# Graph layer on one core: degree count within the first half of G, its second half evicted scaled, norm's small matmuls spread over the blocks

## What is computed

```python
Q = relu(x @ Wq + bq);  V = x @ Wv + bv
# gcn: G = x @ Wg, summed over edges with both degrees' roots
deg  = segment_sum(ones, dst) + 1            # one self loop a node
dinv = rsqrt(max(deg, 1e-12))
gcn  = segment_sum(G[src] * dinv[src] * dinv[dst], dst) + self loop + bg
# former: Q = relu(layer_norm(Q)); H = a scaled square of Q's row sums
cosQ, sinQ = Q * cos(H), Q * sin(H)
out  = (cosQ @ (cosQ.T @ V) + sinQ @ (sinQ.T @ V)) / norm
norm = cosQ @ sum(cosQ) + sinQ @ sum(sinQ) + 1e-10
y = relu(layer_norm(out + gcn + V, gamma, beta))
return layer_norm(x + y)
```

## Time and profile before

| | us |
|---|---|
| median of three runs | 1887.72 |
| lowest and highest run | 1881.73, 1896.17 |
| the profiled execution | 1891.69 |
| its span in the trace | 1889.8 |

### The profile page before, as it was taken

How to read it: one execution, slowest core, us unless ns; L and a number is a source line. 1 busy time by engine, 2 the same in 40 slices (tenths; PEclk the granted TensorE clock), 3 DMA queues, 4 the chain that set the end, 5 groups by cost and what they waited for, 6 DMA issues and landing times.

```text
span 1889.8 us, 27579 instructions
## 1 busy us (share of the span) xinstructions
PE 1642.4 (87%) x7707; PEld 1252.9 (66%) x7707; DVE 1585.2 (84%) x4322; ACT 953.7 (50%) x1789; POOL 1038.4 (55%) x1106
## 2 busy tenths in 40 slices
PE   5888974999999997788888879999899898988995
PEld 4566652777777775565556667767677776777774
DVE  7999975899889897787777878888689888887886
ACT  2222213555555555555555556656456555554554
POOL 0000006777777777677787758878445444444440
PEclk8999985999999999899999989999899898998998
DMA  6445578899888998677777858878566676675762
GB/s 218 160 159 176 173 271 267 281 307 302 290 289 304 302 302 264 196 233 231 247 237 238 246 185 258 257 246 269 167 202 206 197 220 197 195 210 167 220 189 88
DMA packets 179601, 433.16 MB, mean 229 GB/s; under 512 B 24558, under 2 KB 26218, under 8 KB 179432
## 3 DMA queue, kind: packets, MB, share of 16 engines
q0 software_dynamic: 71120, 233.10, 41.0%
q1 hardware_dynamic: 87180, 159.65, 24.8%
q10 hardware_dynamic: 21132, 38.50, 5.5%
HBM read 354.13 MB, written 77.03 MB: 228 GB/s over the span
## 4 chain that ended last, share of the span: by engine, by line
DVE 37%; PE 31%; DMA 11%; issue 7%; ACT 6%; POOL 5%; SPq 1%; DVEq 1%; ACTq 0%; POOLq 0%
DVE stage L787 7%; PE bank L1104 6%; PE bank L1105 6%; PE bank L1106 6%; PE bank L1188 5%; DMA rows<-scaled_g,index_slots 5%; DMA split<-scaled_g,index_slots 5%; PE bank L1190 5%; DVE split L832 4%; POOL split L441 3%; DVE rows L832 3%; DVE stage L783 3%; ACT split L518 3%; DVE one_hot L828 2%; DVE stage L1046 2%
## 5 line engine op out<-in xcount | busy, mean ns | idle before, releaser
L441 POOL DMA_INDIRECT split<-scaled_g,index_slots x490 | 531.5, 1085 | 334.1 <-PE bank L1190 212.4
L441 POOL DMA_INDIRECT rows<-scaled_g,index_slots x392 | 423.8, 1081 | 174.3 <-PE bank L1190 80.0
L1188 PE MATMUL bank<-split,one_hot 128*128 128x512 f32 x882 | 380.5, 431 | 120.4 <-DVE split L832 62.8
L518 ACT CAST split<-split 128x512 fp32r<-128x512 f32 x490 | 301.3, 617 | 356.1 <-PE bank L1190 185.5
L832 DVE TENSOR_TENSOR split<-split 128x512 fp32r<-128x512 f32 x490 | 336.8, 687 | 86.1 <-ACT split L518 84.4
L518 ACT CAST split<-rows 128x512 fp32r<-128x512 f32 x392 | 240.7, 617 | 275.7 <-PE bank L1190 177.2
L1104 PE MATMUL bank<-weights,operands 128*128 128x512 f32 x784 | 323.4, 412 | 4.2 <-DMA operands<-turned_x 4.2
L1188 PEld LDWEIGHTS bank<-split,one_hot 128*128 128x128 f32 x882 | 170.3, 193 | 233.7 <-DVE rows L832 109.0
L1106 PE MATMUL bank<-weights,operands 128*128 128x512 f32 x784 | 317.3, 405 | 0.0
L1105 PE MATMUL bank<-weights,operands 128*128 128x512 f32 x784 | 316.9, 404 | 0.0
L832 DVE TENSOR_TENSOR rows<-rows,split 128x512 fp32r<-128x512 f32 x392 | 270.0, 689 | 50.9 <-ACT split L518 49.3
(11 more groups left out here) (201 smaller groups left out, 2553.9 us busy)
## 6 DMA issues: line engine op xcount, KB each, us to landing
turned_x<-operands SPq DMA_DIRECT2D x49, 512.0 KB, 3.0
operands<-turned_x SPq DMA_DIRECT2D x49, 512.0 KB, 5.9
stage<-values SPq DMA_DIRECT2D x98, 256.0 KB, 4.1
stage<-in_x SPq DMA_DIRECT2D x96, 256.0 KB, 2.7
scaled_g<-nodes SPq DMA_DIRECT2D x49, 256.0 KB, 3.4
own_rows<-scaled_g SPq DMA_DIRECT2D x49, 256.0 KB, 4.1
values<-stage ACTq DMA_DIRECT2D x49, 256.0 KB, 4.1
combine<-values SPq DMA_DIRECT2D x49, 256.0 KB
```

The costliest lines, as they stand in the source:

```text
L441: pool.indirect_dma_start(out=plain(row_ring[k % RING]), out_offset=None, in_=table, in_offset=bass.IndirectOffsetOnAxis(ap=index_slots[:, ...
L518: act.copy(hi_ring[k % SPLIT], plain(row_ring[k % RING])).then_inc(s["chunk_rounded"], 1)
L1188: pe.matmul(gcn_banks[seq % 2][:, :], one_hot[:, slot, :], hi_ring[slot], start=k == 0, stop=False, skip_group_check=True)
```

## The change

- The degree count now takes two units of 18 chunks (10 and 8) a tile, so that 47 units are done within the first 24 tiles (HIST_TILES).
- A half unit's one-hots come from one comparison each on VectorE, against a written-out bf16 counter; the layout is now (j, c), the chunk c innermost. On TensorE the roles are swapped: the one-hot of 49 is the stationary side, that of 128 the moving one, both read at a step of 10 elements. The 49 x 128 result is copied and turned on TensorE.
- `dinv` is ready at tile 26. From tile 28 (SCALED) ScalarE evicts G already scaled; the 28 tiles before are scaled by VectorE, two behind each of tiles 27 to 40, and SyncE stores them two behind each of tiles 28 to 41, and the scaled ones with two tiles' delay. x has four slots from tile 28 on.
- The schedule's set-up moves to tiles 27 to 45, the low parts of Wq and Wv to tiles 3 to 17. The first loads of the QV stage (`first_x_load`) no longer wait for the last tile of G, and their slots in `operands` are other ones. TensorE's wait for `degrees_kept` ahead of QV is gone.
- In OUT, the two small norm matmuls of a block follow that block's products.

```diff
-    HIST = -(-CHUNKS // TILES)
+    HIST = 18
+    HALF = (10, 8)
+    UNITS = -(-CHUNKS // HIST)
+    HIST_TILES = -(-UNITS // 2)
+    SCALED = HIST_TILES + 4
...
             def g_keep(t, n, r):
                 act.wait_ge(s["g_summed"], done(t))
-                act.copy(tile_of(nodes, t)[0:r, :], banks[3 + n][0:r, :]).then_inc(s["g_kept"], 1)
-
+                if t < SCALED:
+                    act.copy(tile_of(nodes, t)[0:r, :], banks[3 + n][0:r, :]).then_inc(s["g_kept"], 1)
+                else:
+                    act.activation(tile_of(nodes, t)[0:r, :], banks[3 + n][0:r, :], ACT.Copy, scale=dinv[0:r, t:t + 1])                        .then_inc(s["g_kept"], 1)
...
+            def table_store(t):
+                if t < SCALED:
+                    sp.wait_ge(s["g_scaled"], t + 1)
+                else:
+                    sp.wait_ge(s["g_kept"], done(t))
+                sp.dma_start(dram_rows(table, t, P), tile_of(nodes, t)).then_inc(s["table_written"], 16)
...
+            for t in range(0, TILES):
+                if t <= WIDE:
+                    g_load(t + 2)
+                if t == WIDE:
+                    g_load(t + 3)
+                if t >= WIDE and t + 4 < TILES:
+                    g_load(t + 4)
+                xt_store(t)
+                if 0 <= t - SCALED < SCALED // 2:
+                    table_store(2 * (t - SCALED))
+                    table_store(2 * (t - SCALED) + 1)
+                if t - 2 >= SCALED:
+                    table_store(t - 2)
+            first_x_load(0)
+            first_x_load(1)
+            table_store(FULL - 1)
+            first_x_load(2)
+            table_store(FULL)
...
-                dve.tensor_tensor(div_hot[half][:, 0:count, 0:TILES],
-                                  iota_bf[:, 0:TILES].unsqueeze(1).to_broadcast([P, count, TILES]),
-                                  cols(dst_div).unsqueeze(2).to_broadcast([P, count, TILES]), ALU.is_equal)
-                for c in range(count):
-                    last = dve.tensor_scalar(mod_hot[half][:, c, :], iota_bf[:, :], column(dst_mod, c0 + c), None,
-                                             ALU.is_equal)
-                last.then_inc(s["bins_ready"], 1)
+                dve.tensor_tensor(div_hot[half][:, 0:TILES, 0:count], counter[:, 0:TILES, 0:count],
+                                  cols(dst_div).unsqueeze(1).to_broadcast([P, TILES, count]), ALU.is_equal)
+                dve.tensor_tensor(mod_hot[half][:, :, 0:count], counter[:, :, 0:count],
+                                  cols(dst_mod).unsqueeze(1).to_broadcast([P, P, count]), ALU.is_equal)\
+                    .then_inc(s["bins_ready"], 1)
...
-                    last = pe.matmul(banks[5][:, 0:TILES], mod_hot[half][:, c, :], div_hot[half][:, c, 0:TILES],
+                    last = pe.matmul(banks[5][0:TILES, 0:P], div_hot[half][:, 0:TILES, c], mod_hot[half][:, :, c],
                                      start=False, stop=False, skip_group_check=True)
...
                 g_product(t, n, r, [0, 1])
-                bins(t, 0)
+                if t < HIST_TILES:
+                    bins(2 * t, 0)
+                    bins(2 * t, 1)
                 g_product(t, n, r, [2, 3]).then_inc(s["g_summed"], 1)
-                bins(t, 1)
+                if t < HIST_TILES and 2 * t + 1 < UNITS:
+                    bins(2 * t + 1, 0)
+                    bins(2 * t + 1, 1)
...
             pe.wait_ge(s["raw_split"], 1 + 2 * B)
-            pe.wait_ge(s["g_kept"], done(FULL))
-            pe.wait_ge(s["degrees_kept"], 1)
...
-                            o_norms(n, slot)
-                            o_product(0, slot, [0, 1])
+                            for b in (0, 1):
+                                o_product(0, slot, [b])
+                                o_norms(n, slot, b)
                         if at == 1:
-                            o_product(0, slot, [2, 3])
+                            for b in (2, 3):
+                                o_product(0, slot, [b])
+                                last = o_norms(n, slot, b)
+                            last.then_inc(s["o_normed"], 1)
```

More of the change, by code:

```diff
@@ L173, in dram_rows, with rows_of, x_slot, x_loads_until @@
             return ap[t * P:t * P + r, :] if isinstance(t, int) else ap[bass.ds(t * P, r), :]
+        def rows_of(t):
+            return TAIL if t == FULL else P
+        WIDE = 28
+        def x_slot(t):
+            return t % 2 if t < WIDE else t % 4
+        def x_loads_until(t):
+            return sum(x_slot(u) == x_slot(t) for u in range(t + 1))
         def column(ap, c):
@@ L730, in between_tiles @@
                 if t == 1:
+                    dve.wait_ge(s["bias_loaded"], 48)
+                    dve.tensor_tensor(bias[:, 1, :], bias[:, 1, :], bias_raw, ALU.add).then_inc(s["bias_summed"], 1)
+                if 3 <= t < 3 + 4 * B and t % 2:
+                    n, b = 1 + (t - 3) // (2 * B), (t - 3) // 2 % B
+                    dve.wait_ge(s["raw_rounded"], n + 1)
+                    dve.tensor_tensor(weights[:, 2 * n - 1, b, :], raws[n][:, b, :], plain(weights[:, 2 * n - 2, b, :]),
+                                      ALU.subtract).then_inc(s["raw_split"], 1)
@@ L731, in between_tiles @@
+                if 0 <= t - (SCALED - 1) < SCALED // 2:
+                    for n in (2 * (t - SCALED + 1), 2 * (t - SCALED + 1) + 1):
+                        g = tile_of(nodes, n)
+                        dve.wait_ge(s["g_kept"], done(n))
+                        dve.tensor_scalar(g, g, column(dinv, n), None, ALU.mult).then_inc(s["g_scaled"], 1)
+                if t == 27:
                     link(dve.tensor_scalar(neg, dst_f, 0.0, 65536.0, ALU.is_lt, ALU.mult))
-                if t == 2:
+                if t == 28:
```

197 lines of the change are left out of this document (102 added, 95 removed).

## The result

The changed kernel takes 2049.65 us (median of 4, 2044.17 to 2051.72) against 1887.08 of the kernel before in the same comparison: ratio 1.0861, 95% interval 1.0831 to 1.0892. The forecast was 1846, with 1895 as its upper end. The kernel became 8.6% slower, where 2.4% faster was forecast.

What follows compares the result with a forecast made beforehand. VectorE was taken to bound G, with TensorE nearly idle through the change-over. Savings of 3 us in G, 40 at the change-over and 2.5 for the clock made 45.5, from 1891.7 to 1846; range 1826 to 1895.

Steps and rivals of the forecast that it cites:

- the price of a count matmul: In G's first half, 846 count matmuls on TensorE at 0.06 us each; 0.027 and 0.10 kept as alternatives.
- the first part: The count in G, tiles 0 to 23: TensorE needs 130.5 us, taken as 133 us for the half.
- the rival of the stepped reads: Count matmuls cost TensorE 0.23 us each, kernel 1987 us, chance 0.08; milder form 0.10 to 0.13, 1880 to 1905, chance 0.13.
- the change-over: From G's end T to round 0's end: POOL at T + 5, chunk 0 at T + 17, end T + 36; 40 us saved.
- VectorE's comparisons: In G's first half, new comparisons run at double rate: 2.24 us a unit, about 0.8 us for 1280 elements.
- The rival at one element in 1.14 ns: New VectorE comparisons in G's first half stay slow, 8.8 us a tile; kernel 1905 to 1924 us; chance 0.06.
- The allowance of 0.1 a tile: In G's first half, added because TensorE and VectorE are near each other with two buffers between them.
- The second half: G's tiles 24 to 48: TensorE's 3.32 us the floor, transfers 3.4 to 4.2 us at some tiles, 94 us in all.
- The rival that transfers bound it at 5 us a tile: Tiles 28 to 48 all at 5 us, G grows some 20 us, kernel 1866 us; chance 0.08.
- the small rival at 0.05: Gathers beside QV's loads keep round 0 or 1 slow, half the 40 us lost; kernel 1866 to 1872; chance 0.05.
- What is won reaches the end: Change-over gain reaches the kernel's end if later rounds run as before; 2.5 us more from the clock not having to recover.
- The norm: In OUT, small norm matmuls behind each block's products: nothing saved on TensorE, put at 0 with -8 and +8 as ends.

Runs made afterwards that it cites:

- With pairs: The changed kernel with both one-hots laid out as pairs of chunks (group, j, 2), read by TensorE at a step of 4 bytes instead of 20: 1842.3 us, ratio 0.9776.
- the run in which one operand stood still: The changed kernel with the moving one-hot of 128 packed (chunk, j), its comparison rewritten, the stationary one left at 20 bytes: 1881.15 us, ratio 0.9966.

## The prediction against the runs, step by step

**What failed: the price of a count matmul**, in the first part. The prediction took 0.06 us "since the stream and not the weight load should set it". The stream does set it, but at these steps it does not run by columns; it runs by 16-byte stretches. The two nearest rows, the old pair and the long matmul, have their moving columns packed or nearly so, and scaling them by the number of columns carried over a property that the change took away. The price was 0.239, and 846 x (0.239 - 0.06) = 151 us. This was the rival of the stepped reads, at 0.23 and with a chance of 0.08. The argument against it, "that a two-byte column needs half the bytes", is what fell: at a step of 16 bytes or more a two-byte column costs a whole stretch. That chance was too small for a side that no row spoke on. The Trainium skill (SBUF — State Buffer, section Door 1: The DMA port swizzle) says that SBUF is read in lines of 16 bytes and that leaving one costs something. The trace agrees with the penalty, and the runs add the size, 1.8 to 2 ns a line. The same section says that two accesses to a line are enough for full bandwidth. Here the measurement decides otherwise for TensorE's moving side: at 8 bytes two columns share a line, and the matmul takes 0.124 us, twice the 0.063 of four columns to a line.

**What neither the forecast nor its rival had: the clock.** The rival gave 1987; the profiled execution took 2049.5. The difference is the clock in the first half, some 62 us, the price at 0.239 instead of 0.23 (8 us), and the change-over (8 us more than forecast), less 16 us in OUT. The prediction took the full clock since TensorE would be busy without a gap. It was busy 346.00 of 346.00 us, and the clock was 0.69. At steps of 16 and 20 bytes the clock is 0.64 to 0.74, at 8 and 4 bytes 0.99. Being busy in the profile did not keep it up. Slow reads alone do not lower it either: at 8 bytes a count matmul costs double, TensorE is busy 146.00 of 146.00 us (23 to 169), and the clock is 0.99. What separates the two cases the runs do not say.

**VectorE's comparisons: right.** Forecast 0.8 us for 1280 elements, measured 0.819, the double rate; the 1024 took 0.684. The prediction also let line 787 speak for its side: less the same fixed 105 ns, its 0.172 for 128 elements is 0.52 ns each, which is the double rate as well. The rival at one element in 1.14 ns (1924) is out, and it came true only in the run in which one operand stood still.

```profile
L846 DVE TENSOR_TENSOR stage<-nodes,combine 128x1280 bf16<-128x1280 bf16 x47 | 38.5, 819 | 0.0
L846 DVE TENSOR_TENSOR stage<-nodes,combine 128x1024 bf16<-128x1024 bf16 x47 | 32.2, 684 | 0.0
```

**The first half without the stride.** With pairs it took 146.8 us against 133 forecast. The matmul was right (0.063 for 0.06), but a tile takes 6.23 us instead of 5.5. TensorE's own 3.32 + 36 x 0.063 is 5.6. The rest shows in the timeline as distances of 0.32 instead of 0.23 us from a count to a product or back, and as one short wait for a comparison in most tiles (0.21 us). The allowance of 0.1 a tile for two engines so near each other was too small.

**The second half: right.** Forecast 94 us; measured 92.9 in the change (369.6 to 462.5) and 93.0 with pairs (169.2 to 262.2), at a transfer share of 0.91 and 0.92. The rival that transfers bound it at 5 us a tile did not come.

**The change-over: right in kind, too large by 8 us.** From the last product of G to the end of round 0 before took 76.5 us, now 44.2; the forecast had 36. All engines' timeline of the changed kernel, the answer to the earlier trace rows:

```profile
462.48 0.40 PE L1156 MATMUL bank<-split,operands 128*106 128x512 f32 x1
463.63 0.33 SPq L311 DMA_DIRECT2D scaled_g<-nodes  x1
465.04 0.47 PE L1154 MATMUL bank<-weights,operands 128*128 128x512 f32 x1 [2.17 <-issue]
470.95 0.20 POOL L468 COPY dst_slots<-dst_cols 128x18 f32 x1 [462.73 <-issue]
481.47 0.40 PE L1247 MATMUL bank<-split,one_hot 128*128 128x512 f32 x1
...
506.71 0.48 PE L1154 MATMUL bank<-weights,operands 128*128 128x512 f32 x1
```

The last store is issued 1.2 us behind the product (0.5 forecast), POOL starts at T + 8.5 instead of T + 5, TensorE waits 2.17 us for QV's first input where under 1 us was forecast, and the first chunk is multiplied at T + 19 instead of T + 17. From there to the end of round 0 it is 25.2 us, where 19 were forecast. The run with the stores first took away most of POOL's delay and won nothing. So the term most mis-sized is the rate of the round (6 of the 8 us), not its start (2). Beside it stand transfer engines at 0.76 to 0.78, shared by gathers and x loads, and a clock of 0.84 where the forecast had 1.00; which of the two slows the round, no run separates. It may be the small rival at 0.05 that had gathers beside QV's loads, in a milder form.

**What is won reaches the end: right.** Rounds 1 to 16 took 5.1 us less than before (2.5 forecast for the clock), rounds 17 to 36 1.4 more.

**The norm: wrong in size, outside its own ends.** 0 within 8 was forecast, -12 to -18 came. The forecast reckoned TensorE's own time, and that part holds: a block's product and its pair stand 0.91 us apart where product and product are 0.69, thus 0.22 for each exposed pair of loads, four times a tile as forecast. What was missing is the clock: with the run ahead of the products more of them run at the lower level, 67 us against 37. The earlier trace rows show a tile in which the clock stayed up; the windows' 0.92 in the earlier trace rows for OUT, against 0.97 in the rounds before, was the sign that something lowers it there. It stood in the prediction's own rows and was not asked about.

**Balance.** Against the forecast of -45.5 us the span came out at +157.8, so 203 us off: 213.6 first half (151 price, 62 clock, and about 0 for the rest), -1 second half, +8 change-over, -1 rounds, -16 norm. Without the first term the forecast of 1846 would have stood: the kernel with pairs took 1842.3. But it stands by luck, by misses that nearly cancel: 14 us in G's first half and 7 at the change-over not won that were forecast, and 21 us won in OUT (539.5 against 560.9) that were not.

## What to carry to other kernels

Before a matmul operand is laid out at a step, count the 16-byte stretches that its columns touch, on the moving side above all: here each costs about 1.9 ns, so two-byte columns cost no more than the long matmul's rate at 4 bytes apart, double at 8 and fourfold at 16 and more. VectorE's comparison wanted its operands to walk in the innermost step, and a run of two elements was enough for that, so a layout in pairs serves both engines. Where a window's granted clock is a few hundredths below the full one, look for the places at which it falls: here moving eight short matmuls from behind a wait to behind long ones won 12 to 18 us, nearly all of it through the clock.

## What the runs showed of the hardware that was not expected

- At a step, TensorE's moving side is charged by 16-byte stretches: 0.237 to 0.239 us for 128 bf16 columns at 16 and 20 bytes, 0.124 at 8, 0.063 at 4; on the weight side 0.095 for 49 at 20 bytes. Eighteen of them took the same 4.31 us at a granted clock of 0.82 and of 0.50: this cost does not follow the clock.
- An engine that is busy for all of 346 us can be granted 0.69 of its clock, with counts at 0.239 us; with counts at 0.124 it was granted 0.99, busy all the same. In the run with the counts spread it was 0.50 in one execution and, by its span's mean of 0.974, far higher in the other, at the same time of the kernel. Why two executions of one kernel differ so is open.
- In OUT the clock fell to the lower level eleven times in eleven rounds, seven times at a wait of 1.9 us and four times behind one of 1.0; with products ahead of the small matmuls, four to six times.
- A change from fp32 products to bf16 counts and back costs 0.44 us at the lower clock level, in the change and in the run with the counts spread; 0.40 us of idle time stand ahead of the product's weight load. With pairs the distances at the change are 0.32 and 0.34 us instead of 0.23, so it is no matter of the stepped layout alone. Its cause is open.
